# Own row numbers for nodes without edges, and 7 KB rows for two DRAM buffers

## The reference

```python
src, dst = sorted by dst, 206250 edges          # 6250 of them are loops
h0 = gat_conv(x, W0, as0, ad0, b0, row=src, col=dst)
nr, nc = row[col], col[col]                     # edges of the second convolution
h1 = gat_conv(x, W1, as1, ad1, b1, nr + loops, nc + loops)
x = x + layernorm(concat(h0, h1) + x) * gamma + beta
x = x + moe_ffn(layernorm(x))                   # 8 experts, 2 of them for each node
# gat_conv: per node and head a softmax over the edges that end in it,
#           and the weighted sum of the projected rows of their sources
```

## Time and profile before

| | us |
|---|---|
| median of 3 runs | 3315.36 |
| their range | 3311.18 to 3315.59 |
| profiled execution, its time | 3312.09 |
| its span | 3310.3 |
| PE busy | 1930.1 |
| DVE busy | 2118.3 |
| POOL busy | 2015.1 |
| ACT busy | 1201.3 |

### The profile page before, as it was taken

How to read it: one execution, slowest core, us unless ns; L and a number is a source line. 1 busy time by engine, 2 the same in 40 slices (tenths; PEclk the granted TensorE clock), 3 DMA queues, 4 the chain that set the end, 5 groups by cost and what they waited for, 6 DMA issues and landing times.

```text
span 3310.3 us, 33785 instructions
## 1 busy us (share of the span) xinstructions
PE 1930.1 (58%) x8606; PEld 1397.7 (42%) x8607; DVE 2118.3 (64%) x3742; ACT 1201.3 (36%) x2081; POOL 2015.1 (61%) x2011
## 2 busy tenths in 40 slices
PE   4500000016767776776677677301345999999998
PEld 2400000003333433433343344101345999999997
DVE  8546766557887788788778878746773433333333
ACT  3313444433343334334333433412452333333332
POOL 4677777777777777777777777736663222222222
PEclk8855555558888888888888788655556999999999
DMA  9725458743344444444444444397564222222222
GB/s 290 160 56 144 151 162 154 219 150 122 122 121 143 131 122 122 153 121 121 143 131 122 121 153 122 115 230 129 157 189 145 36 36 37 37 37 36 37 35 32
DMA packets 242423, 400.68 MB, mean 121 GB/s; under 512 B 78399, under 2 KB 197843, under 8 KB 235289
## 3 DMA queue, kind: packets, MB, share of 16 engines
q1 hardware_dynamic: 163417, 247.16, 23.1%
q0 software_dynamic: 77792, 151.99, 22.4%
q10 hardware_dynamic: 1120, 0.52, 0.1%
HBM read 207.94 MB, written 191.63 MB: 121 GB/s over the span
## 4 chain that ended last, share of the span: by engine, by line
POOL 45%; PE 23%; issue 16%; DVE 7%; DMA 4%; SPq 2%; ACT 1%; DVEq 1%; POOLq 0%; ACTq 0%
POOL AR L726 43%; PE ps L1136 10%; PE ps L1142 9%; DMA out<-AR,idb 2%; POOL AR L714 1%; DVE AR L1225 1%; PE ps L1104 1%; SPq L544 1%; SPq L580 1%; POOL adstart L698 1%; ACT AR L981 1%; PE ps L1116 1%; PE ps L1033 1%; PE ps L1127 1%; PE ps L1095 1%
## 5 line engine op out<-in xcount | busy, mean ns | idle before, releaser
L726 POOL DMA_INDIRECT AR<-tables,idx x1536 | 1450.5, 944 | 468.1 <-issue 468.1
L1062 PE MATMUL ps<-AR 128*128 128x408 f32 x2584 | 976.8, 543 | 781.5 <-DVE AR L1440 781.5
L1062 PEld LDWEIGHTS ps<-AR 128*128 128x128 f32 x2584 | 526.1, 205 | 1232.0 <-issue 809.9
L806 POOL DMA_INDIRECT out<-AR,idb x105 | 195.5, 1862 | 581.6 <-issue 548.4
L1372 DVE TENSOR_TENSOR_SCAN AR<-ps,AR 128x512 f32<-128x512 f32 (+1 forms) x486 | 518.7, 1141 | 4.0
L905 ACT ACTIVATE ps<-AR 128x512 f32<-128x512 f32 x432 | 254.3, 596 | 471.1 <-DVE AR L1372 471.1
L911 ACT COPY AR<-AR 128x1984 f32<-128x1984 f32 (+1 forms) x108 | 423.2, 3966 | 0.7 <-DVE AR L1372 0.7
L1136 PEld LDWEIGHTS ps<-AR 128*128 128x128 f32 x3360 | 393.9, 193 | 6.5 <-DVE AR L1785 1.2
L1136 PE MATMUL ps<-AR 128*128 128x128 f32 x3360 | 394.5, 276 | 0.8 <-DVE AR L1785 0.8
L1366 DVE TENSOR_TENSOR AR<-AR,ps 128x3968 f32<-128x3968 f32 (+1 forms) x54 | 371.0, 6871 | 0.2
L892 ACT ACTIVATE ps<-AR 128x248 f32<-128x248 f32 (+1 forms) x54 | 20.5, 380 | 705.9 <-DVE AR L1350 705.9
(11 more groups left out here) (306 smaller groups left out, 1952.1 us busy)
## 6 DMA issues: line engine op xcount, KB each, us to landing
state<-AR SPq DMA_DIRECT2D x53, 2232.0 KB, 9.6
AR<-tables,idx POOLq DMA_INDIRECT x1585, 2.6
AR<-in_L_ffn_W SPq DMA_DIRECT2D x16, 1024.0 KB, 9.3
AR<-placed SPq DMA_DIRECT2D x105, 129.0 KB, 2.1
AR<-adstart SPq DMA_DIRECT2D x53, 248.0 KB, 4.0
adstart<-zero SPq DMA_DIRECT2D x26, 496.0 KB, 4.4
tables<-AR SPq DMA_DIRECT2D x49, 136.0 KB, 2.6
hbd<-eb2b SPq DMA_DIRECT2D x7, 896.0 KB, 9.5
```

The source lines that it names most:

```text
L726: pool.indirect_dma_start(out=G[s][:, j, 0:ROWT], out_offset=None, in_=table_rows, in_offset=bass.IndirectOffsetOnAxis(ap=idx[:, s, j:j + ...
L806: pool.indirect_dma_start(out=out, out_offset=bass.IndirectOffsetOnAxis(ap=idb[:, s, :], axis=0), in_=ys[:, s, :], in_offset=None, bounds_ ...
L1062: mm = T.matmul(ps[c][:, 0:w], onehot[c][:, a, :], table_cols[:, a * w:(a + 1) * w], start=(a == 0), stop=(a == LEV - 1))
```

## The change

Two edits. First, the row number of a node without edges is its own number in place of the clamped position: with `has` = 1 for a node with edges and 0 for the others, it is (position - 1 - node) * `has` + node. Second, `hbd` and `xkept` have, in DRAM, the layout that they have in SBUF: a group is 128 rows of 7 * 256 floats, so that each partition's 7168 bytes stand together, where there were seven rows of 1024 bytes apart from each other.

```diff
-        hbd = dram("hbd", [NP, D])
+        hbd = dram("hbd", [NG, P, GRP * D])
-        xkept = dram("xkept", [NP, D])
+        xkept = dram("xkept", [NG, P, GRP * D])
...
                 def biased(g):
-                    sp.dma_start(halves[g], hbd[g * GRP * P:(g + 1) * GRP * P, :].rearrange("(t p) d -> p t d", p=P)).then_inc(biased_loaded[BIASED_IN[g][0]], 16)
+                    sp.dma_start(halves[g].rearrange("p t d -> p (t d)"), hbd[g]).then_inc(biased_loaded[BIASED_IN[g][0]], 16)
...
-                        sp.dma_start(hbd[g * GRP * P:(g + 1) * GRP * P, :].rearrange("(t p) d -> p t d", p=P), norm_again).then_inc(biased_stored, 16)
+                        sp.dma_start(hbd[g], norm_again.rearrange("p t d -> p (t d)")).then_inc(biased_stored, 16)
...
-                        sp.dma_start(xkept[g * GRP * P:(g + 1) * GRP * P, :].rearrange("(t p) d -> p t d", p=P), X[:, g * GRP:(g + 1) * GRP, :]).then_inc(x_rows_stored, 16)
+                        sp.dma_start(xkept[g], X[:, g * GRP:(g + 1) * GRP, :].rearrange("p t d -> p (t d)")).then_inc(x_rows_stored, 16)
...
-                            sp.dma_start(X[:, g * GRP:(g + 1) * GRP, :], xkept[g * GRP * P:(g + 1) * GRP * P, :].rearrange("(t p) d -> p t d", p=P)).then_inc(x_loaded[g], 16)
+                            sp.dma_start(X[:, g * GRP:(g + 1) * GRP, :].rearrange("p t d -> p (t d)"), xkept[g]).then_inc(x_loaded[g], 16)
...
                 V.tensor_tensor(fin_[:, 2, :], fin_[:, 0, :], fin_[:, 1, :], ALU.is_gt)
-                V.tensor_scalar(fin_[:, 3, :], fin_[:, 0, :], -1.0, 0.0, ALU.add, ALU.max)
-                dd()
-                V.tensor_copy(node_index[:, 2 + k, :], fin_[:, 3, :])
+                V.scalar_tensor_tensor(fin_[:, 3, :], fin_[:, 0, :], -1.0, nid[:, :], ALU.add, ALU.subtract)
+                dd()
+                V.tensor_tensor(fin_[:, 3, :], fin_[:, 3, :], fin_[:, 2, :], ALU.mult)
+                dd()
+                V.tensor_tensor(node_index[:, 2 + k, :], fin_[:, 3, :], nid[:, :], ALU.add)
                 V.tensor_scalar(bare[:, k, :], fin_[:, 2, :], -1.0, BIG, ALU.add, ALU.mult)
```

## The result

| | before | after |
|---|---|---|
| median, us | 3314.63 (4 runs) | 3285.89 (4 runs) |
| range, us | 3311.18 to 3315.59 | 3284.56 to 3287.19 |
| profiled execution, its span, us | 3310.3 | 3282.7 |
| DMA packets | 242423 | 220919 |

The ratio is 0.9915, 95% interval 0.9898 to 0.9932: 28.7 us faster by the medians, 27.6 us by the spans. The forecast of 3285 lay 0.9 us beside the median. The profiled execution of before, 3312.09 us, is not among the four behind its median (nor among the three of the table ahead of the prediction, though the text there says so); the changed kernel's is, with 3284.56.

The account below looks back on a forecast made before the run. POOL's gather issues bound the loop; behind it, the last store waits on SP's full queue and slow gathers of line 771. Gains of 23.8 and 4.6 us make 28.4: 3283.7 us, median forecast 3285, range 3279 to 3307.

Parts of the forecast that it names:

- The first DVE instruction of batch 51: After the loop's last gather: it lands 1 us later beside 7 KB loads, so DVE starts at 2166.1 (+1.0).
- Line 1529: Where DVE needs the border rows of the last batch: starts at 2207.5 instead of 2231.32, 23.8 us gained.
- DVE's arm of the step: Before line 1529: without waits of 17.61, 1.28 and 6.27 us, plus 1.0, DVE is ready at 2207.2.
- The arm of the border rows: Before line 1529: ACT's copy, store issue, landing of 8.7 to 9.6 us and fetch bring the rows at 2206.6 to 2207.5.
- The wait on line 771: DVE's wait that ended at 2257.90: the last gather lands in 3.2 us instead of 7.81, 4.6 us gained.
- The next wait, on line 764: DVE's wait for group 1's gathers: some 1.4 us late, but beside 5 us of ACT's work, so zero.
- the sum of 28.4 us: Whole kernel: 23.8 us at line 1529 plus 4.6 us at the wait on line 771, giving 3283.7 us.
- Part 2: The 7 KB pieces of `hbd` and `xkept`: zero in the loop, nothing of their own to the main term.
- the main term: The start of line 1529 in the last batch, 23.8 us gained.
- Rival (b): Behind the loop: own rows fetch as slowly as the shared one, store lands at 2229, 3316 to 3320 us; chance 0.05.
- Rival (a): Loop's last gathers starve beside 7 KB loads, last lands at 2187, 7.5 us of gain left, 3306 us; chance 0.17.
- the 32 packets a microsecond that the forecast took: Queue 0's rate beside 8 KB pieces, at which 224 waiting gather packets take 7 us and the last lands at 2166.

Follow-up runs that it names:

- the control: The changed kernel with both edits and nothing else, run again beside the kernel before on one chip: 3283.51 us, ratio 0.9916.
- part 1 alone: Against the changed kernel, own row numbers kept, `hbd` and `xkept` back in the old layout of 1 KB rows: 3286.22 us, ratio 0.9921.
- the first four experiments: The control (3283.51 us), part 1 alone (3286.22), new layout without own row numbers (3305.07), changed kernel with POOL's group 4 gathers ahead of the border rows' store (3283.30).

## Why the prediction was right, step by step

**The first DVE instruction of batch 51**: forecast 2166.1, measured 2165.07. The delay behind the last gather is right: 2158.41 to 2165.07 is 6.7 us where it was 5.6, 1.1 us later as against 1.0 in the sum. It is hidden by a last gather that was itself issued 1.1 us earlier; other executions with the same loop have it at 2158.64 to 2160.51, so that is the scatter from run to run and no effect of the change.

**Line 1529** (now 1531): forecast 2207.5, measured 2206.33. From the start of batch 51 that is 41.3 us, forecast 41.4. DVE's arm of the step came out: no wait for `hbd`, and DVE gets there by its own work. The arm of the border rows was too long: the store was issued 0.03 us behind ACT and POOL started the fetch 7.9 us later, where the sum had 9.3 to 10.2 (its landing of 8.7 us stands in no row; the earlier trace rows has 7.7, 9.6 and 13.7). So the rows landed at 2204.2 and not at 2206.6 to 2207.5. The sum had the two arms late at once; since the step takes the later one, this cost the forecast nothing. 25.0 us are gained, 1.1 of them the scatter.

**The wait on line 771**: forecast 4.6 us shorter. From line 1531 to its end it is 21.33 us, before 2257.90 - 2231.32 = 26.58: 5.25 us shorter. The last gather landed after 2.6 us, not 3.2; the term is 0.65 too small.

**The next wait, on line 764**: forecast zero, and this step was wrong. I had POOL 1.4 us late here and hid that beside ACT's work. The prediction does not show how it came to 1.4; it is near the 1.7 us that are left of its 4.6 when the 2.9 us of DVE's wait for ACT are taken off once. DVE's gap from the one row to the other is 29.5 us after and 25.1 before, so the gathers are 4.4 us later relative to DVE; the 3.30 us that DVE waited for ACT at line 1612 shrank to 0.36, which covers 2.9. The remaining 1.5 us is lost: at line 1614 after is 28.7 us ahead, 2288.08 to 2259.35, with 30.2 us at the wait before. The amount of 1.4 was right here and the word "hidden" was not. In the control and with part 1 alone the same gap is 30.6 us, and 2.6 us are lost. What hides a delay must not be counted again for what is left of it.

So the sum of 28.4 us agrees with the 28.7 at line 1614 partly by luck, because errors cancel: 1.1 from scatter and 0.65 from the landing on one side, 1.5 given back on the other. By the end 1.1 of the 28.7 is lost again, 27.6 by the spans, with no wait of the change in it: from line 1614 to the end the profiled executions of before, after and the first four experiments take 1022.0 to 1025.2 us. For an execution like the profiled one the forecast was 3283.7 us, and 3284.56 was measured. That the medians are 28.7 apart, nearer to the sum than the 27.6 of the spans, is scatter of four runs each.

**Part 2** was forecast to give nothing of its own to the main term: with part 1 alone the time is 3286.22, with both 3283.51, and at line 1531 of the profiled executions the two are 0.9 us apart. Right. Rival (b) was wrong in its sum. It let a 7 KB piece go for a gather packet of 0.8 us and so stretched the gathers to 2215; the queues between 2168 and 2204 show 0.64 us a gather packet (0.63 x 16 x 36 / 570) and the same 16 of them a microsecond as before. The gathers were through at about 2206, the store landed at 2218 instead of 2229, and the 3 us of loss at line 1529 were 8 us of gain. If the row number had done nothing, the change would still have been faster.

**Rival (a)**, starving gathers, did not come. The queues of after between 2164 and 2165, as the earlier trace rows:

```profile
q1 hardware_dynamic: 69, 0.38, 96.2%
q0 software_dynamic: 32, 0.05, 14.1%
```

Two of the loads' packets to one of the gathers, and 46 to 47 two microseconds earlier. In "DMA: Bandwidth & Descriptors" of the Trainium skill, section "Queues, rings and completion order", a turn is a packet of typically 9 to 17 descriptors; at 7 KB these rows do not show a turn of that many pieces for one gather packet, as those at 8 and 17.8 KB did not; how long a turn of either queue is, they can't tell.

One thing the prediction misread in the earlier trace rows: queue 0's packets there are not those of gathers. POOL was issuing line 797's scatters, which write `placed`, from 2360.36 to 2380.18. So the 32 packets a microsecond that the forecast took came from a row of another kind. In the microsecond behind the earlier trace rows, 2370 to 2371, the 4 KB load moved 97 packets and queue 0 none, although the scatters issued at 2366.20, 2367.48 and 2368.76 took 8.3 to 8.8 us to land. That is what starving beside 4 KB pieces would look like, but whether their packets were ready by then the trace doesn't show; it stays open, as above.

## What to carry to other kernels

Lanes whose result is masked away still cost their fetch: give them rows of their own rather than one row for all; eight rows for 128 lanes were as cheap here. Where the DMA engines are fully busy at a third of the rate seen a moment before, look for the queue whose packets take long, and divide its share by its packets. When a wait is shortened, go on to the next two waits of the same engine on the same slower one, and take off each piece of cover only once.

## What the runs showed of the hardware that I had not expected

- Gathers of 576-byte rows: share of the DMA engines 0.22 to 0.25 for 58 to 59 GB/s with own, far or eight rows; 0.72 to 0.73 for 56 to 60 where 128 readers of a gather share one; 1.02 for 44 GB/s where all gathers share it. That the far rows are as cheap as neighbours, and eight as cheap as 128, was open before.
- Loads of 7 KB pieces and the gathers beside them ran at 402 GB/s, those of 1 KB, with own rows too, at a lower rate. Busy time by stretch with part 1 alone:

```profile
2165.00:2185.00 20.00, 0.00 (x0) 0.00 (x0) 18.42 (x18) 6.77 (x12) 15.12 (x17) 0.50 1.09 344
```

- For the same bytes and with the engines full in each case, 896 pieces a load kept SP at its seven and four issues for 34 us, 256 pieces for 18, 128 for 10 to 12. With 128 pieces SP was through after 12 us also in the layout alone, where the loads of `hbd` then took 49 us in the median to land: they waited in the queue and not at SP. With 896 pieces it was 34 us where the engines moved 344 GB/s and 60 us in before, where they moved 122. So SP is held by the number of pieces, and with many of them also by how fast they are worked off.
